# The causal mask of the first attention: added to the scores by TensorE, or written as zeros into the exponentials by GpSimd

## Reference

```python
scores = jnp.einsum('bhqd,bhkd->bhqk', q, k) / jnp.sqrt(jnp.float32(hd))
causal = jnp.tril(jnp.ones((N, N), dtype=bool))
scores = jnp.where(causal[None, None], scores, -jnp.inf)
weight = jax.nn.softmax(scores, axis=-1)
out = jnp.einsum('bhqk,bhkd->bhqd', weight, v)
```

## Time and profile before

| | us |
|---|---|
| median of 3 runs | 2696.15 (2688.54 to 2734.21) |
| the profiled execution, its own time | 2693.72 |
| its span, from the first to the last instruction | 2692.0 |
| TensorE busy in the span | 2394.0 |
| VectorE busy | 1749.8 |
| ScalarE busy | 1249.9 |
| GpSimd busy | 566.8 |

### The profile page before, as it was taken

The page is one execution under the profiler, slowest core; times in us unless marked ns, Lnnn a source line. Parts: engine busy times, 40 slices in busy tenths (PEclk is TensorE's granted clock), DMA queues, the critical chain, the costliest instruction groups (busy, mean ns, idle before and its releaser), DMA issues. The chain is left out here.

```text
span 2692.0 us, 42224 instructions
## 1 busy us (share of the span) xinstructions
PE 2394.0 (89%) x16394; PEld 1498.7 (56%) x16394; DVE 1749.8 (65%) x2066; ACT 1249.9 (46%) x2372; POOL 566.8 (21%) x480
## 2 busy tenths in 40 slices
PE   4959999969999999999999869979969999999947
PEld 2748888846555444444444347758745555555515
DVE  3745444555767878888886043422259999999954
ACT  2422222204555767777788522212215655656531
POOL 1110000030000000000000002220036766666650
PEclk8979999977999999999999889989989999999978
DMA  3771000034321211000000020015562222220024
GB/s 123 238 231 48 32 32 31 0 62 85 82 61 38 58 45 30 30 30 21 29 18 15 13 67 1 0 48 116 192 145 47 51 65 65 65 63 10 8 67 144
DMA packets 133182, 168.60 MB, mean 63 GB/s; under 512 B 60736, under 2 KB 70592, under 8 KB 129920
## 3 DMA queue, kind: packets, MB, share of 16 engines
q1 hardware_dynamic: 129536, 153.45, 21.5%
q10 hardware_dynamic: 3456, 12.58, 1.5%
HBM read 114.19 MB, written 51.64 MB: 62 GB/s over the span
## 5 line engine op out<-in xcount | busy, mean ns | idle before, releaser
L710 ACT ACTIVATE a_ex<-a_ps_s 128x512 f32<-128x512 f32 (+3 forms) x1280 | 620.0, 532 | 331.3 <-PE a_ps_s L793 249.3
L913 DVE TENSOR_REDUCE a_mx_part<-a_ps 128x2 f32<-128x1024 f32 (+3 forms) x576 | 584.0, 1043 | 132.2 <-PE a_ps L739 129.7
L1206 ACT ACTIVATE a_ex<-a_ps_s 128x512 f32<-128x512 f32 (+3 forms) x640 | 318.3, 532 | 285.9 <-PE a_ps_s L1267 160.3
L793 PE MATMUL a_ps_s<-a_q,a_k 50*128 50x512 f32 (+3 forms) x1152 | 395.9, 419 | 2.8 <-ACT a_ex L710 2.8
L1181 POOL TENSOR_TENSOR a_acc<-a_acc,a_ex 128x512 f32<-128x512 f32 (+3 forms) x288 | 352.0, 1222 | 95.8 <-ACT a_ex L1206 75.0
L739 PE MATMUL a_ps<-a_k,a_q 48*128 48x512 f32 (+3 forms) x1152 | 346.0, 418 | 27.4 <-DVE a_low_q L898 14.8
L837 PE MATMUL a_ps_o<-a_ex,a_v 128*32 128x256 f32 (+1 forms) x5120 | 361.8, 364 | 4.9 <-ACT a_o L680 4.2
L1331 DVE TENSOR_REDUCE a_mx_part<-a_ps 128x2 f32<-128x1024 f32 (+2 forms) x320 | 336.1, 1054 | 32.4 <-PE a_ps L1233 22.8
L793 PEld LDWEIGHTS a_ps_s<-a_q,a_k 50*128 50x128 f32 x1152 | 180.7, 188 | 206.4 <-ACT a_ex L710 144.2
L1230 PE MATMUL a_ps<-a_k,a_q 96*128 96x512 f32 (+3 forms) x640 | 211.6, 397 | 44.1 <-DMA a_q<-q 22.9
L1372 DVE TENSOR_TENSOR a_acc<-a_acc,a_ex 128x512 f32<-128x512 f32 (+3 forms) x288 | 248.8, 864 | 2.3 <-ACT a_ex L1206 0.2
(11 more groups left out here) (218 smaller groups left out, 3898.8 us busy)
## 6 DMA issues: line engine op xcount, KB each, us to landing
a_q<-q SPq DMA_DIRECT2D x192, 64.0 KB, 2.3
a_k<-k SPq DMA_DIRECT2D x24, 512.0 KB, 5.2
a_q<-q SPq DMA_DIRECT2D x24, 512.0 KB, 7.2
q<-p_oh SPq DMA_DIRECT2D x32, 256.0 KB, 2.4
q<-p_ol SPq DMA_DIRECT2D x32, 256.0 KB, 2.6
o<-a_o SPq DMA_DIRECT2D x32, 256.0 KB, 2.2
a_v<-v SPq DMA_DIRECT2D x12, 512.0 KB, 7.6
mlp_raw<-in_wup SPq DMA_DIRECT2D x5, 1024.0 KB, 5.0
```

The source lines that it names most:

```text
L710: act.activation(ex[unit % NE][:, h % 2, off:CH], ps_s[n % 3][:, off:CH], ACT.Exp, scale=SCALE)\
L793: pe.matmul(ps_s[n % 3][:, off:CH], k_st[r0:r0 + KM, g, t * P:(t + 1) * P], q_st[b % NQ][r0:r0 + KM, h // HALVES, off:CH], start=True, sto ...
L913: dve.tensor_reduce(part[:, 2 * p:2 * p + 2, i - TPC * c, kc], bank[:, :, 0:w], AX.X, ALU.max).then_inc(taken1, 1)
L1206: act.activation(ex[s % NE][:, h, off:CH], ps_s[n % 3][:, off:CH], ACT.Exp, scale=SCALE)\
```

## The change

In the gathered step TensorE's four mask multiplications go, and the signal moves to the last of the eight products. ScalarE's exponentials are then unmasked. GpSimd writes zeros above the diagonal into each pair's exponentials, in place (`affine_select`, 1024 elements a partition), once ScalarE has written both heads, and raises a semaphore `masked`. TensorE's values of a gathered step wait for it, and are no longer cut into two halves around the second pair's scores of the next step: all stand behind that pair. GpSimd's queue, which was only the 16 multiplications and subtractions, is now written out by steps: at step s first the subtraction of S = s-5, then the multiplication of S = s-2, then the two selects if s is gathered. One constant tile (`low_k`) is no longer made.

```diff
-            for j in range(NCH * KT):
-                k = j % KT
+            def mask_diagonal(s):
+                b, t = STEP_LIST[s]
+                for p in range(PAIRS):
+                    unit = s * PAIRS + p
+                    tiles = ex[unit % NE][:, :, :].rearrange("p e (j q) -> p (e j) q", j=TPC)
+                    pool.wait_ge(exp_done, s * HG + 2 * (p + 1))
+                    pool.affine_select(out=tiles, in_=tiles, compare_op=ALU.is_ge, fill=0.0, base=0,
+                                       pattern=[[0, 2 * TPC], [1, P]], channel_multiplier=-1).then_inc(masked, 1)
...
+            for s in range(STEPS0 + PREP + 5):
+                if s - 5 in PREP_AT:
+                    low(*PREP_AT[s - 5])
+                if s - 2 in PREP_AT:
+                    divide(*PREP_AT[s - 2])
+                if s < STEPS0 and gathered(RUNS[STEP_LIST[s][0]][0], STEP_LIST[s][1]):
+                    mask_diagonal(s)
...
-                        pe.matmul(ps_s[(n + e) % 3][:, tile], k_st[r0:r0 + KM, g, c * CH + j * P:c * CH + (j + 1) * P],
-                                  q_st[b % NQ][r0:r0 + KM, h // HALVES, tile], start=j == 0, stop=False)
-                sel = mask["k"][0]
-                for part in range(HALVES):
-                    for e in range(2):
-                        r0 = (2 * p + e) % HALVES * ROWS
-                        cols = ps_s[(n + e) % 3][:, :].rearrange("p (j s q) -> p s j q", j=TPC, s=HALVES)[:, part]
-                        mm = pe.matmul(cols, sel[r0:r0 + ROWS, part, :], low_k[r0:r0 + ROWS, :, :],
-                                       start=False, stop=part == HALVES - 1)
-                        if part == HALVES - 1:
+                        mm = pe.matmul(ps_s[(n + e) % 3][:, tile],
+                                       k_st[r0:r0 + KM, g, c * CH + j * P:c * CH + (j + 1) * P],
+                                       q_st[b % NQ][r0:r0 + KM, h // HALVES, tile], start=j == 0, stop=j == TPC - 1)
+                        if j == TPC - 1:
                             mm.then_inc(scores2, 1)
...
                 pe.wait_ge(exp_done, (s + 1) * HG)
+                if gathered(c, t):
+                    pe.wait_ge(masked, PAIRS * (b + 1))
...
-                    if s > 0:
+                    if s - 1 in LAST_STEP and p == PAIRS - 1:
+                        times_v(s - 1, 0, CH)
+                    elif s > 0 and s - 1 not in LAST_STEP:
                         times_v(s - 1, p * CH // PAIRS, (p + 1) * CH // PAIRS)
```

More of the change, by code:

```diff
@@ L506, in attention @@
         zr = [sb(f"zr{i}", [P, ZN]) for i in range(NZ)]
-        low_k, low_q = [sb(f"low_{n}", [P, TPC, P // HALVES], F32R) for n in "kq"]
+        low_q = sb("low_q", [P, TPC, P // HALVES], F32R)
         o_raw, z_raw = sb("o_raw", [P, CH]), sb("z_raw", [P, CH])
@@ L522, in attention @@
         scores2, exp_done, pv_done = sem("scores2"), sem("exp_done"), sem("pv_done")
+        masked = sem("masked")
         staged = sem("staged")
@@ L665, in _, with divide, low @@
             pool.wait_ge(blank, NCH * HALVES)
-            for j in range(NCH * KT):
-                k = j % KT
+            def mask_diagonal(s):
[6 more added lines that the diff above has]
+                                       pattern=[[0, 2 * TPC], [1, P]], channel_multiplier=-1).then_inc(masked, 1)
+            def divide(c, k):
+                j = c * KT + k
                 pool.wait_ge(raw_in, 32 * (j + 1))
                 pool.tensor_tensor(o_raw[:, :], o_raw[:, :], z_raw[:, :], ALU.mult).then_inc(normed, 1)
+            def low(c, k):
+                j = c * KT + k
                 pool.wait_ge(o_high, j + 1)
                 pool.tensor_tensor(ol[:, k, :], o_raw[:, :], oh[:, k, :].bitcast(F32), ALU.subtract).then_inc(o_low, 1)
+            for s in range(STEPS0 + PREP + 5):
[5 more added lines that the diff above has]
+                    mask_diagonal(s)
         @block.scalar
@@ L846, in spin @@
                     pe.matmul(out, mask["k"][0][:, 0, :], k_st[:, 0, 0:CH], start=True, stop=True)
-            pe.wait_ge(part_init, 4)
+            pe.wait_ge(part_init, 3)
             for n in TICKS[-1]:
@@ L896, in _ @@
                 dve.memset(part[:, :, :, :], NEG).then_inc(part_init, 1)
[L897 to L900, removed]
+            dve.tensor_copy(low_q[:, :, :], mask["q"][1][:, :].unsqueeze(1).to_broadcast([P, TPC, P // HALVES]))\
+                .then_inc(part_init, 1)
+            dve.wait_ge(part_init, 3)
             def maxima(n):
```

## The result

The changed kernel took 2754.90 us in the median of 4 runs (2733.37 to 2772.60); the kernel before, on the same chip, 2699.73 (4 runs, 2688.54 to 2734.21). The ratio is 1.0205 [1.0151, 1.0259]: slower, by some 55 us, where 2699 was forecast with a range that ended at 2734. Whether the loss is over 2% these runs leave open. All ratios here leave out runs over 1.5% above the fastest of the same kernel, so they understate what the clock costs.

The account below looks back on a forecast made before the run. TensorE, busy 98 of 100 us, and its loop with ScalarE were taken as the bound. Gathered steps -8.5 us, late loads in GpSimd's queue +11 and the end +0.7 gave about +3: 2699 us, range 2670 to 2734.

Parts of the forecast that it names:

- the first part: First attention: TensorE is busy 98 of 100 us at the full granted clock, so a microsecond no longer needed can count.
- sum of +3: Whole kernel: 8.5 us gained in gathered steps, 11 lost to late loads, 0.7 lost at the end; about 3 us slower.
- The last part: Signs to look for: selects of 1.1 to 1.3 us, TensorE waits of 0.4 and 4 to 6 us, possible clock falls.
- the rivals: Three other outcomes: slow selects, 2779 us (0.11); nothing waits, 2673 (0.15); mask gone but nothing won, 2708 (0.08).
- the selects are slow: GpSimd's selects run at the two-input rate, 2.5 us each; TensorE waits, 83 us lost, 2779 us; chance 0.11.
- The mask multiplications go: Gathered step: 0.29 us of issue a pair leaves the TensorE-ScalarE loop twice; 0.58 us a step, 18.6 us over 32.
- The values in one piece: Step behind a gathered one: 32 value instructions together let the next scores come 0.14 us sooner, 4.5 us in all.
- The selects: GpSimd's select of 1024 elements takes 1.15 us, within 1.0 to 2.5.
- The wait for them: TensorE's values stand 0.39 us for GpSimd; 0.15 us gained a step in chunks 2 and 3, 0.4 in 0 and 1.
- GpSimd's queue: Late-loaded L669 multiplications ahead of the selects delay TensorE's values at steps 23, 39 and 31: 4.1, 5.5, 1.4; 11 us lost.
- The end: Last run's values wait for the last select, 1.25 us more behind exponentials that come 0.58 earlier: 0.7 us lost.

Follow-up runs that it names:

- e4: The changed kernel without the selects and without TensorE's wait for them, no mask computed, scores times 0.001: 2759.84 us, 1.0200 of the kernel before.
- e1: The kernel before without its mask multiplications, values still in two halves, no mask computed, scores times 0.001: 2745.77 us, 1.0139 of the kernel before.
- e2: The kernel before with the values of gathered steps in one piece, mask still on TensorE: 2723.41 us, 1.0102 of the kernel before.
- f1: The changed kernel with two overwritten filler multiplications ahead of the second pair, in gathered steps and in steps behind: 2696.63 us, 0.9991 of the kernel before.
- e3: The changed kernel with four extra, overwritten multiplications of 256 columns ahead of each gathered pair's products: 2724.40 us, 1.0084 of the kernel before.
- f6: The changed kernel with one filler multiplication instead of two at each of two idle places: 2698.12 us, 0.9995 of the kernel before.
- g1: The changed kernel with the second pair's first head multiplied before the wait, plus two fillers in the step behind: 2712.57 us, 1.0058 of the kernel before.
- f3: The kernel before without mask multiplications, scores times 0.001, values in halves, two fillers ahead of the gathered step's second pair: 2676.33 us, 0.9924 of the kernel before.
- h1: The kernel before with the second pair's first head, products and mask, ahead of the wait for the first exponential: 2686.15 us, 0.9957 of the kernel before.
- f2: The changed kernel with two fillers only ahead of the gathered step's second pair: 2732.23 us, 1.0093 of the kernel before.

## Why the prediction was wrong

**The step that failed** is in the first part: "So a microsecond that TensorE no longer needs can count", with 98 of 100 us busy at the full clock. The clock was taken as given, like the length of an operation. It was the kernel's own work that held it: with 0.58 us of mask issue a gathered step gone and the values moved into one piece, TensorE's clock went to half in spells of up to 120 us. That is the +80 us of the stage, against a sum of +3. The last part names a clock that falls, but behind waits of 4 to 6 us for GpSimd, without a price, a chance or a rival. Those waits came out short, and only one spell, of 8 us at 753, began behind one of them (2.25 us); the clock fell in gathered steps and steps behind that had no such wait, and it fell as far in e4, which has none at all. None of the rivals is the mechanism found. That the time came past 2734 on the side of "the selects are slow" is no support for it: the select was as fast as forecast.

**The mask multiplications go: right at the full clock.** Second pair 1.35 (1.34), next step 2.58 (2.52). In e1 the step is 0.43 shorter than before, of 0.58 forecast for the mask alone; over 32 steps that is 14 us instead of 18.6. The 1.63 between the pairs, told there of 22 of 24 gathered steps, the trace has in 23.

**The values in one piece: wrong in sign.** -0.14 a step was forecast; e2 shows +0.24. The working of it replaced two pieces by one and left out that the halves stood between scores and blocks that wait for banks.

**The selects: right.** 1.15 was forecast, and the group of the changed kernel has 64 of 1097 ns. The Trainium skill ("GPSIMD Engine Reference", section 4.1) has one-input work at roughly line rate; with 1.10 us the trace agrees: it is nearer to the 0.85 that the prediction estimated from that page for one input than to the 2.2 for two.

```profile
L675 POOL TENSOR_SCALAR_AFFINE_SELECT a_ex<-a_ex 128x1024 f32<-128x1024 f32 x64 | 70.1, 1097 | 559.4 <-ACT a_ex L735 559.4
```

**The wait for them: right in time, wrong in cause.** The values came at 4.46 (4.43) and the step at 5.47 (5.43), so 0.11 a step was left of the 0.15 forecast. But e4 has them at 4.46 without any select. The last select ends at 4.29 from the step's start, and the work ahead of the values on TensorE ends about as late. A replay can give the right time through the wrong wait; only the run without the wait tells.

**GpSimd's queue: two of three places right, the size off.** 11 us in three waits was forecast. TensorE's waits of the changed kernel, 600 to 1620 us (total, times, longest), and the three for GpSimd:

```profile
PE a_ps_s L832 <- ACT a_ex L735: 11.8, 28, 0.7
PE a_ps L764 <- DVE a_mx_part L935: 7.9, 15, 0.9
PE a_ps_o L858 <- POOL a_ex L675: 3.9, 3, 2.3
```

```profile
690.98 1.08 PE L858 MATMUL a_ps_o<-a_ex,a_v 128*32 128x128 f32 x32 [0.51 <-POOL a_ex L675]
...
751.38 1.08 PE L858 MATMUL a_ps_o<-a_ex,a_v 128*32 128x128 f32 x32 [2.25 <-POOL a_ex L675]
...
1615.71 1.08 PE L858 MATMUL a_ps_o<-a_ex,a_v 128*32 128x128 f32 x32 [1.17 <-POOL a_ex L675]
```

Steps 23 and 39 wait 0.51 and 2.25 us, where 4.1 and 5.5 were forecast; step 31, with 1.4, does not wait; the third wait is the last run's, the next term. So the queue cost 2.8 us: the data came earlier. Before, the multiplications of these three steps started 6.0, 2.7 and 9.4 us behind the first products of their gathered steps, now 3.1, 0.5 and 7.1. That of step 39 started at 747.87 instead of 750.97:

```profile
747.87 1.28 POOL L682 TENSOR_TENSOR a_o_raw<-a_o_raw,a_z_raw 128x512 f32<-128x512 f32 x1 [22.93 <-DMA a_z_raw<-z]
749.10 2.14 POOL L675 TENSOR_SCALAR_AFFINE_SELECT a_ex<-a_ex 128x1024 f32<-128x1024 f32 x2
```

**The end: right.** From the last exponentials to the copy-out it is 2.44 us against 1.21, so 1.23 more (1.25 forecast); the pairs there are 1.35 apart instead of 1.63.

**The sum without the clock** can be estimated from f1, which holds it. Among runs at the same mean clock, 0.948, f1 takes 2692 to 2694 us and the kernel before 2683 to 2687, so f1 is some 7 us behind; its steps are 0.30 longer than the changed kernel's, 9.6 us over 32. At that clock the changed kernel would so be within a few us of the one before, where +3 was forecast. Errors of both signs are in that sum (the mask and the one piece against the loads), so a part of the agreement is luck; but none of its terms was off by more than some 12 us (the one piece), and the stage grew by 80.

**D, chance,** is not nothing: the kernel before had a run at a mean clock of 0.912 itself. But the runs of the changed kernel lie at 0.904 to 0.920, the 12 of f1 at 0.938 to 0.950, and no two of them meet.

**Still open:** how thin the work may become before the clock falls. e3 (the mask's columns, on fewer rows, at another place), f6 (half the fillers) and g1 (the same work earlier) lie between and give no rule. Nor are TensorE's pauses the rule. Its waits for the first exponential were these in the kernel before, at the full clock, where the changed kernel has 11.8 us in 28:

```profile
PE a_ps_s L807 <- ACT a_ex L710: 13.8, 28, 0.7
```

They are gone in f1, f3 and h1, which keep the clock, but in f2 too, and in g1 all but 0.5 us, and these two don't. Nor was it shown what ends a spell.

## What to carry to other kernels

In a kernel that TensorE bounds, look at the granted clock of each stretch as a resource that the work itself pays for: before counting removed multiplications as a gain, find where they stood, and whether the engine pauses for another one beside them. When a kernel with less work is slower and one engine's busy time has grown, compare the clock over the same stretch first; a filler in the pause is the quickest test. And test a reordering by itself, even if it looks like a free addition to the main edit: here it was a loss at the full clock and a second cause of the lower one.

## What the runs showed of the hardware

TensorE's granted clock fell from 2.4 to 1.2 GHz in gathered steps and the ones behind, with pauses of some 0.4 to 0.5 us, in an engine that was 97 to 98 of 100 us busy, and stayed there for 60 us (924 to 985) and 120 us (1125 to 1245) while the engine was as busy (39.85 of 40 us at 0.50). Taking 256 of its 16394 instructions away cost 1.4% (e1); adding two fillers at two places to the changed kernel gave 2% back (f1). The Trainium skill, "TensorE: Matmul & The Clock Gate", section "A second HAM failure mode: psum-queue depth-cycling", has a kernel in which short pauses between groups of multiplications let the clock swing between its two levels; these traces agree in the swing between two levels at short pauses, with the spells above as their number, in float32 and with pauses for other engines; but the kernel before has such pauses too (0.56 us in step 95) and keeps the clock there.
